# A mixture-of-experts stage on one core: eight places for outputs, gathers two blocks ahead, spare blocks shared out

## The reference, cut to what matters

```python
def expert_step(y, params):              # for each of the 32 experts
    wgu, wd, cw = params
    gu = x @ wgu.T                       # 2048 x 384
    g, u = jnp.split(gu, 2, axis=-1)
    h = jax.nn.silu(g) * u               # 2048 x 192
    y = y + h @ wd.T * cw[:, None]       # cw: the token's weight for this expert, mostly 0
    return (y, None)
```

## Time and profile before

| what | value |
|---|---|
| median of three runs | 1644.93 us (1644.88 to 1650.45) |
| the profiled execution's own time | 1643.69 us |
| its span, first to last instruction | 1641.5 us |
| TensorE busy | 1463.0 us (89%) |
| DMA engines' share, queue of SyncE | 33.3% |
| DMA engines' share, queue of GpSimd | 26.8% |
| expert stage, first gather to last scatter's start | 968 to 1596 us of the span |

### The profile page before, as it was taken

The page is one execution under the profiler, slowest core; times in us unless marked ns, Lnnn a source line. Parts: engine busy times, 40 slices in busy tenths (PEclk is TensorE's granted clock), DMA queues, the critical chain, the costliest instruction groups (busy, mean ns, idle before and its releaser), DMA issues.

```text
span 1641.5 us, 33300 instructions
## 1 busy us (share of the span) xinstructions
PE 1463.0 (89%) x11189; PEld 823.3 (50%) x11190; DVE 954.7 (58%) x1885; ACT 711.5 (43%) x1295; POOL 770.7 (47%) x683
## 2 busy tenths in 40 slices
PE   3799999999999999999995369989998999999980
PEld 1466666644444444445553226545555666666640
DVE  6877777786757576624889664333333444444437
ACT  5344344455464646434554334334333444444430
POOL 2465454540010101233566245556655876766754
PEclk9899999999999999999997579999999999999995
DMA  6132211279677777511111058999999998888868
GB/s 233 52 113 77 68 26 38 59 240 317 225 258 233 257 230 261 179 55 52 54 54 54 1 191 216 247 250 281 257 256 259 163 167 146 147 148 146 148 101 308
DMA packets 97101, 269.51 MB, mean 164 GB/s; under 512 B 15152, under 2 KB 15568, under 8 KB 91920
## 3 DMA queue, kind: packets, MB, share of 16 engines
q1 hardware_dynamic: 61424, 182.75, 33.3%
q0 software_dynamic: 35616, 85.99, 26.8%
HBM read 158.83 MB, written 101.47 MB: 159 GB/s over the span
## 4 chain that ended last, share of the span: by engine, by line
PE 57%; DMA 14%; DVE 12%; issue 6%; POOL 6%; ACT 3%; SPq 1%; DVEq 0%; POOLq 0%; ACTq 0%
PE bank L855 13%; DMA acc<-X,WA 12%; PE bank L535 10%; PE bank L876 7%; PE bank L667 6%; PE bank L673 6%; PE bank L696 6%; PE bank L846 3%; POOL ARENA L1623 1%; DMA ARENA<-acc 1%; POOL ARENA L1618 1%; PE bank L776 1%; DVE ARENA L994 1%; DVE ARENA L1227 1%; PE bank L524 1%
## 5 line engine op out<-in xcount | busy, mean ns | idle before, releaser
L855 PE MATMUL bank<-ARENA,XT 128*128 x1908 | 368.0, 328 | 3.3 <-DVE XT L1305 1.4
L1749 POOL DMA_INDIRECT acc<-X,WA x159 | 253.0, 1591 | 170.4 <-ACT X L1343 142.7
L855 PEld LDWEIGHTS bank<-ARENA,XT 128*128 128x128 f16 x1908 | 181.1, 98 | 130.0 <-issue 17.5
L1305 DVE COPY XT<-bank 128x1024 f16<-128x1024 f16 x159 | 109.9, 691 | 172.1 <-PE bank L846 170.8
L876 PE MATMUL bank<-ARENA,XT 128*128 x795 | 199.7, 382 | 7.3 <-issue 5.5
L1343 ACT ACTIVATE ARENA<-ARENA 128x512 f16<-128x512 f32 (+2 forms) x128 | 90.5, 709 | 252.4 <-DVE ARENA L1077 133.0
L1743 POOL DMA_INDIRECT XT<-x_rows,WA x159 | 157.1, 988 | 55.4 <-issue 40.5
L535 PE MATMUL bank<-WA,XT 128*128 128x512 f16 (+1 forms) x768 | 137.5, 333 | 22.2 <-DVE WA L918 19.4
L535 PE MATMUL bank<-XT,STG 128*128 128x512 f16 x640 | 150.2, 382 | 0.0
L1605 POOL TENSOR_TENSOR rstd<-mv,mhalf 128x1 f32<-128x1 f32 x44 | 15.1, 342 | 282.2 <-DVE mv L924 282.2
L1315 DVE SCALAR_TENSOR_TENSOR XT<-bank,XT 128x192 f32<-128x192 f32 x159 | 66.4, 418 | 139.3 <-ACT XT L1582 133.1
(11 more groups left out here) (218 smaller groups left out, 2347.2 us busy)
## 6 DMA issues: line engine op xcount, KB each, us to landing
w_scratch<-WA SPq DMA_DIRECT2D x64, 640.0 KB, 3.9
ARENA<-w_scratch SPq DMA_DIRECT2D x32, 1280.0 KB, 7.7
ARENA<-w_exp SPq DMA_DIRECT2D x48, 640.0 KB, 5.2
WA<-w_exp SPq DMA_DIRECT2D x16, 640.0 KB, 5.2
ARENA<-ARENA SPq DMA_DIRECT2D x64, 128.0 KB, 2.3
acc<-ARENA SPq DMA_DIRECT2D x18, 256.0 KB, 3.0
x_rows<-ARENA SPq DMA_DIRECT2D x17, 256.0 KB, 2.4
STG<-xT SPq DMA_DIRECT2D x8, 512.0 KB, 4.5
```

The costliest lines, as they stand in the source:

```text
L855: mm = pe.matmul(d, xTb[k.u % 2][:, a * KD + kd, :], weights(sl, b, kd * 2 * DFF, 2 * DFF), start=(a, b, kd) == (0, 0, 0), stop=(a, b, kd) ...
L1305: dve.tensor_copy(xTb[k.u % 2].rearrange("p c n -> p (c n)"), bank[k.u % 2][:, :].bitcast(F16)).then_inc(xt_sb, 1)
L1749: pool.indirect_dma_start(acc[i % 2], bass.IndirectOffsetOnAxis(blkidx[:, i:i + 1], 0), yD[i % 4], None, compute_op=ALU.add).then_inc(y_ou ...
```

## The change

Three edits belong together. `yD` gets eight places instead of four, and only two semaphores (one for each accumulator) count the landings. GpSimd's order becomes ten gathers first, and then gather(i+10), scatter(i). And the tables are made with `spare` = round((159 - 15.5 - needed blocks) / 32) extra blocks for each of the experts, so that the blocks past the needed ones no longer all stand behind expert 31. The spare blocks of an expert hold padding rows alone. The number of blocks stays 159.

```diff
+AHEAD = 2
-        yD = [X[:, j, :] for j in range(4)]
+        yD = [X[:, j, :] for j in range(8)]
...
             pe.matmul(bank[2][0:EXPERTS, 0:1], upper[0:EXPERTS, :], nb[0:EXPERTS, 0:1], start=True, stop=True)
+            pe.matmul(bank[2][0:EXPERTS, 1:2], ones[0:EXPERTS, 0:EXPERTS], nb[0:EXPERTS, 0:1], start=True, stop=True)
...
-            step(dve.tensor_scalar(nb[one, 0:1], cnt[one, :], MAGIC, None, ALU.subtract))
-            dve.tensor_scalar(short[one, :], nb[one, 0:1].to_broadcast([EXPERTS, P]), -float(EXPERTS), base[one, :],
-                              ALU.mult, ALU.add).then_inc(nb_ready, 1)
+            dve.tensor_scalar(nb[one, 0:1], cnt[one, :], MAGIC, None, ALU.subtract).then_inc(nb_ready, 1)
+            own.did(dve.tensor_scalar(pos1[one, :], iotap[one, :], 1.0, None, ALU.add))
             one_hots(2)
             places(3)
             dve.wait_ge(end_ready, 1)
-            step(dve.tensor_copy(endc[one, :], bank[2][one, 0:1]))
-            dve.tensor_scalar(ended[one, 0:NBLK], iotab[one, :], endc[one, :], None, ALU.is_ge).then_inc(ended_ready, 1)
-            own.did(dve.tensor_scalar(ends[0:1, :], bank[3][0:1, 0:EXPERTS], 1.0, None, ALU.add))
+            step(dve.tensor_scalar(spare[one, :], bank[2][one, 1:2], -1 / EXPERTS, (NBLK - 0.5 * (EXPERTS - 1)) / EXPERTS, ALU.mult, ALU.add))
+            step(dve.tensor_scalar(spare[one, :], spare[one, :], MAGIC, MAGIC, ALU.add, ALU.subtract))
+            own.did(dve.scalar_tensor_tensor(more[0:1, :], iota[0:1, :], 1.0, spare[0:1, :].to_broadcast([1, EXPERTS]), ALU.add, ALU.mult))
+            step(dve.scalar_tensor_tensor(endc[one, :], pos1[one, :], spare[one, :], bank[2][one, 0:1], ALU.mult, ALU.add))
+            own.did(dve.tensor_scalar(ended[one, 0:NBLK], iotab[one, :], endc[one, :], None, ALU.is_ge))
+            step(dve.tensor_scalar(cnt[one, :], nb[one, 0:1], spare[one, :], -float(EXPERTS), ALU.add, ALU.mult))
+            dve.tensor_scalar(short[one, :], cnt[one, :].to_broadcast([EXPERTS, P]), base[one, :], None, ALU.add).then_inc(ended_ready, 1)
+            own.did(dve.scalar_tensor_tensor(ends[0:1, :], more[0:1, :], 1.0, bank[3][0:1, 0:EXPERTS], ALU.add, ALU.add))
...
             def y_evac(k):
                 act.wait_ge(blk_done, k.i + 2)
-                if not k.before(4):
-                    act.wait_ge(y_out[k.u % 4], k.use(4) * 16)
-                copy(yD[k.u % 4], bank[6 + k.u % 2][:, :], 1 / (WS * WS)).then_inc(y_sb, 1)
+                if not k.before(8):
+                    act.wait_ge(y_out[k.u % 2], k.use(2) * 16 - 48)
+                copy(yD[k.u % 8], bank[6 + k.u % 2][:, :], 1 / (WS * WS)).then_inc(y_sb, 1)
...
             def scatter(i):
                 pool.wait_ge(y_sb, i + 1)
                 if i >= 2:
-                    pool.wait_ge(y_out[(i - 2) % 4], (i - 2) // 4 * 16 + 16)
+                    pool.wait_ge(y_out[i % 2], i // 2 * 16)
...
-            for i in range(NG):
+            for i in range(NG + AHEAD):
                 gather(i)
             for i in range(NBLK):
-                if i + NG < NBLK:
-                    gather(i + NG)
+                if i + NG + AHEAD < NBLK:
+                    gather(i + NG + AHEAD)
                 scatter(i)
```

More of the change, by code:

```diff
@@ L205, in build @@
         cnt, nb, endc = r.take([1], F32), r.take([2], F16), r.take([1], F32)
+        spare, pos1, more = r.take([1], F32), r.take([1], F32), r.take([EXPERTS], F32)
         ended = r.take([160], F16)
@@ L279, in build @@
         slots_ready, slotsT_ready, slotsT_sb, blk_ready = sem("slots_ready"), sem("slotsT_ready"), sem("slotsT_sb"), sem("blk_ready")
-        w_in, xg_in, y_out = sem("w_in"), [sem(f"xg_in{i}") for i in range(NG)], [sem(f"y_out{i}") for i in range(4)]
+        w_in, xg_in, y_out = sem("w_in"), [sem(f"xg_in{i}") for i in range(NG)], [sem(f"y_out{i}") for i in range(2)]
         xt_ready, xt_sb, gu_ready, sg_ready, h_ready, h_hi, h_lo, ht_ready, ht_sb, blk_done, y_sb = (sem(n) for n in (
@@ L504, in _ @@
                 load_expert(e)
-            for j in range(4):
-                sp.wait_ge(y_out[j], 16 * len(range(j, NBLK, 4)))
+            for j in range(2):
+                sp.wait_ge(y_out[j], 16 * len(range(j, NBLK, 2)))
             for t in range(NT):
@@ L1747, in scatter @@
                 if i >= 2:
-                    pool.wait_ge(y_out[(i - 2) % 4], (i - 2) // 4 * 16 + 16)
-                pool.indirect_dma_start(acc[i % 2], bass.IndirectOffsetOnAxis(blkidx[:, i:i + 1], 0), yD[i % 4], None,
-                                        compute_op=ALU.add).then_inc(y_out[i % 4], 16)
+                    pool.wait_ge(y_out[i % 2], i // 2 * 16)
+                pool.indirect_dma_start(acc[i % 2], bass.IndirectOffsetOnAxis(blkidx[:, i:i + 1], 0), yD[i % 8], None,
+                                        compute_op=ALU.add).then_inc(y_out[i % 2], 16)
             pool.wait_ge(tables_ready, 1)
```

## The result

The changed kernel takes 1652.9 us (median of 20 runs, 1642.06 to 1660.52) against 1647.3 us (1642.86 to 1651.88, 20 runs). The ratio is 1.0038, 95% interval 1.0023 to 1.0053: slower, by 0.2 to 0.5%. I had forecast 1620 against 1644.9, a gain of 25 us; none of it came. The profiled execution took 1645.96 us (span 1644.1); it lies 7 us under the median of its runs, so what follows shows a little less than the typical loss.

The account below looks back on a forecast made before the run. Late scatters beside weight loads were taken to cost TensorE 36.7 us in the expert stage. 1643.7 - 27.0 (less stall) + 0.8 (tables) + 1.5 (end) = 1619.0, with the median of before 1620; range 1607 to 1637 us.

Parts of the forecast that it names:

- What bounds the kernel: In the expert stage before 1262 us, late scatters and gathers cost TensorE 36.7 us; after that TensorE itself bounds.
- ledger of debt, payment and buffer: In GpSimd's scatter chain loads add backlog, each block repays 0.46 us, buffering holds 17.5 us; 9.7 us stall TensorE.
- price c of a load: Backlog that one weight load adds to GpSimd's scatter chain: taken as 3.0 us, for 28 loads 84 us.
- reading (c): Load price from two scatters of one accumulator standing 10.6 us apart: 4.2 us for one load.
- rival C: Each load costs the scatter chain 3.6 to 4.18 us, the stall returns nearly whole: 1637 to 1653 us; chance 0.08.
- (a): Load price from the 50 scatters between 1047.5 and 1257.3 us, with 22 loads in between: 2.4 us.
- (b): Load price from the expert stage's whole first part, with all 28 loads: 2.8 us.
- rival D: Each load costs the scatter chain above 4.18 us, between blocks 15 and 124: slower, 1656.6 us at 4.3; chance 0.05.
- Sharing: Two padding blocks per expert move the last load from block 68 to 124, which pays 57 us of 84.
- Eight places and earlier gathers: Backlog of scatters and gathers that TensorE doesn't feel rises from 10.2 to 17.5 us; gathers bind first.
- Tables: After `end_ready` VectorE does eight small operations instead of three before the one-hot rows: 0.8 us more.
- End: Scatter backlog left after the last block, before the accumulators are read back: 1.5 us, range 0 to 2.

Follow-up runs that it names:

- Tiny loads: The changed kernel with each of the 28 weight loads in the expert stage cut from 1,280 KB to 64 KB: 1609.9 us, ratio to before 0.978.
- four accumulators: The changed kernel with scatters waiting for the one four before, not two; half of the experts' part is missing from the output: 1609.8 us.
- spaced loads in the old order: The kernel before with every second of the 28 loads cut to 64 KB, so 14 full loads stand 4.9 blocks apart: 1628.1 us.
- pairs: The changed kernel with its loads issued two by two, when the later one's slot comes free: 1633.7 us, ratio to before 0.992.

## Why the prediction was wrong

**What bounds the kernel: right.** The ledger of debt, payment and buffer gives 1638 to 1640 for the places alone (measured 1637.2), 1655 to 1662 for the sharing alone (1655.6; this one with c = 4.0, which was read off the result), and the floor of 1609 is where the runs without a debt lie (1609.8 to 1610.7). Tiny loads and four accumulators show both ends of it, the cause and the chain that carries it.

**The price c of a load: wrong, and the step that failed.** I took 3.0 between readings of 2.4, 2.8 and 4.2, "nearer to the mean over all". The changed kernel has 4.2 by its median, 4.0 by its profiled run: (37.1 + 56.8 + 17.5) / 28. With the 4.2 of reading (c), which stood in the rows of before, the same sum gives 28 x 4.2 - 74.3 = 43.3 us stalled and 1644.9 - 36.7 + 43.3 + 2.3 = 1654, against 1652.9 measured. This was rival C, to which I gave 0.08. The error was in the choice, not in the rows. The readings (a) and (b) are means over crowded loads, and the change removes just that crowding; (c) was the reading of a load with room around it, the state that the change makes the rule. I wrote so ("pulls towards (c)") and then averaged all the same. That c depends on spacing was only argued then. Now it is shown, from both sides: 4.2 for spaced loads in the old order, 3.5 for pairs in the new one.

The trace of before could have settled it, for its loads are not equally crowded. From 1047 to 1258 us five loads are issued 11.7 to 15.7 us after the one before them (1068.6, 1109.8, 1173.5, 1221.9, 1242.9). GpSimd waits for them in front of a scatter for 4.12, 3.23, 4.40, 4.24 and 4.29 us (through ScalarE's copy, which waits for the landing). The 14 loads issued at most 9.2 us after the one before them leave 1.7 to 3.6 us, most of them near 2.5, and one nothing over 1.5. Two neighbours, for the loads issued at 1068.6 and 1077.3:

```profile
1078.59 1.59 POOL L1749 DMA_INDIRECT acc<-X,WA  x1 [4.12 <-ACT X L1343]
```

```profile
1087.29 1.59 POOL L1749 DMA_INDIRECT acc<-X,WA  x1 [2.56 <-ACT X L1343]
```

The prediction saw these five, under rival D ("five loads of before, alone in their time, would have to be the rule"). With the loads 14 to 23 us apart they are the rule. Its reason for the low readings, that crowded loads overlap the same scatters, does not hold: nearly every crowded load has a wait of its own, only a shorter one. Why it is shorter is not shown. It may be that GpSimd, just held up by the load before, has fewer DMAs in flight beside the next one.

Two smaller slips change nothing. A part of each loss is the clock, which the ledger books to the loads: PEclk 0.98 over 277 us before and 0.99 over 485 us after are an estimated 5 us each. And the 17.5 us of buffer take a down product as 1.08 us long in one term and as 1.24 in another, a difference of 0.16 us.

**Sharing: mis-sized through c.** It pays 56 blocks x 0.458 = 25.6 us more, and raises the price of 28 loads by 1.2 to 1.5 us each, 34 to 42 us. That is a net loss, where I had a gain. The last load is issued at 1469.6 us, where I had about 1445; the larger stall before it makes the difference.

**Eight places and earlier gathers: right.** 7.2 us by the medians (11 by the ratio) against 7.3 of the ledger. Gathers do bind first: ScalarE's wait went to 1.1 us and late gathers became the wait of TensorE. GpSimd's new order costs nothing that shows.

**Tables: right.** From `end_ready` to the first one-hot VectorE takes 951.98 - 950.52 = 1.46 us against 0.50, 0.96 more where I had 0.8:

```profile
950.52 0.15 DVE L1270 TENSOR_SCALAR WA<-bank 32x1 f32<-32x1 f32 x1
...
951.98 1.84 DVE L1230 TENSOR_SCALAR ARENA<-WA 128x512 f16<-128x512 f16 x5
```

**End: within its range.** The backlog was paid back before the last block, and the last scatter starts 2.4 us later than before (1598.73 against 1596.29), of which 1.9 are the later start of the first block. The tables account for 0.96 of these. In the rest TensorE's clock has a part: in the 16 us around the first down product PEclk reads 0.73 (972 to 988 us), where before had 0.82 (971 to 987).

## What to carry to other kernels

When a change alters how crowded a cost is, take its price from the instances that already look like the new state, not from the mean: here five loads among 22 told 4 us, the mean over all told 2.8. Where bulk loads share the DMA engines with a chain of small, latency-bound DMAs, it is worth trying them in several DMAs with rows as short as, or shorter than, those of the chain, as long as the load, which gets longer, still comes in time. And look for the chain itself: two more accumulators took away a loss that no spreading of the traffic did.

## What the runs showed of the hardware

A load of 1,280 KB in ten DMAs of 1,024 B rows disturbs a concurrent accumulating scatter less than one DMA with 10,240 B rows (1611.9 us against 1652.9; with ten DMAs the scatters land in 8.0 us at most), at the price of 10.1 us in place of 6.7. A load that follows another within 10 us holds the scatters up less than one that stands alone, 2.4 us against 4.3 in pairs. An accumulating scatter of 128 rows of 2,048 B lands in 4.8 us with no load beside it and took up to 10.4 us under a lone load (the kernel before with every second load cut), and GpSimd's issue of it takes 1.59 us in either case. DMA engines at 0.92 busy still carried the whole stage at TensorE's pace, so a share near 1 was no proof of a throughput limit. After a wait of 6.4 us for weights TensorE's granted clock read 0.50 for 5 us.
